# Sorted edge records scattered as rows of 16 words into tables of 64-byte rows

## What is computed

```
x = x + gnn0(norm(x), src, dst)        # two layers: mean of x[dst] over the edges of src, dense, norm, silu
x = x + experts(norm(x))               # 8 experts, two per node, 256 -> 1024 -> 256
x = x + gnn1(norm(x), src, dst, w)     # sum of w * x[src] over the edges of dst, dense, norm, gelu
x = x + half(x)                        # top half of each block of 512 rows through a dense pair
```

## Time and profile before

| | us |
|---|---|
| median of 3 runs | 7271.44 |
| lowest and highest | 7270.54, 7273.53 |
| span of the profiled execution | 7265.6 |
| busy in it: TensorE | 3646.1 |
| POOL | 3769.2 |
| VectorE | 2657.8 |
| ScalarE | 899.9 |

### The profile page before, as it was taken

One profiled execution on the slowest core, in us unless ns is written; L12 is line 12 of the kernel. 1 busy time (PEld: TensorE's weight loads), 2 busy tenths in 40 slices (PEclk: granted clock), 3 DMA queues, 4 the chain that ended last, 5 costly groups with the idle time before them and its releaser, 6 DMA issues. The chain is left out here.

```text
span 7265.6 us, 61921 instructions
## 1 busy us (share of the span) xinstructions
PE 3646.1 (50%) x13991; PEld 2632.2 (36%) x13992; DVE 2657.8 (37%) x6350; ACT 899.9 (12%) x2400; POOL 3769.2 (52%) x3797
## 2 busy tenths in 40 slices
PE   4112974444544445444431222299992455555729
PEld 1001543333333333333221000178881334333517
DVE  5115864444433444444340000011114455555661
ACT  0000950000003000000230000022221100000322
POOL 4772036666663666666537777700005566666321
PEclk7556987777777777777665555599996678787859
DMA  3000113333321333332011000022214233333250
GB/s 136 1 0 30 21 49 92 92 92 92 91 61 61 90 92 91 92 92 83 21 58 59 4 2 8 4 75 81 83 57 137 88 90 91 90 91 91 70 162 18
DMA packets 290147, 497.59 MB, mean 68 GB/s; under 512 B 99253, under 2 KB 182880, under 8 KB 290048
## 3 DMA queue, kind: packets, MB, share of 16 engines
q0 software_dynamic: 163264, 345.19, 16.7%
q1 hardware_dynamic: 125696, 150.28, 6.3%
q10 hardware_dynamic: 1088, 1.05, 0.1%
HBM read 487.50 MB, written 92.89 MB: 80 GB/s over the span
## 5 line engine op out<-in xcount | busy, mean ns | idle before, releaser
L970 PE MATMUL sum_sums<-sum_got,sum_onehot 128*128 x4992 | 1613.7, 484 | 1690.7 <-DVE acc L1132 1360.6
L902 POOL DMA_INDIRECT sum_got<-xn,edge_row x1568 | 1541.5, 983 | 1138.9 <-issue 451.4
L970 PEld LDWEIGHTS sum_sums<-sum_got,sum_onehot 128*128 128x128 f32 x4992 | 1166.3, 244 | 2121.9 <-issue 1915.4
L1132 DVE TENSOR_TENSOR acc<-acc,sum_sums 128x257 f32 (+1 forms) x2496 | 1052.7, 422 | 1777.8 <-remote 1241.3
L902 POOL DMA_INDIRECT sum_got<-h,edge_row x784 | 754.4, 962 | 453.3 <-issue 228.4
L1270 POOL DMA_INDIRECT table<-rec,addr x784 | 802.8, 1024 | 298.5 <-issue 277.4
L1866 PE MATMUL moe_f_ps_y<-xb,moe_f_hT 128*128 128x256 f32 x1792 | 478.8, 399 | 317.3 <-issue 317.2
L1850 PE MATMUL moe_f_ps_h<-moe_f_xT,xb 128*128 128x256 f32 x1792 | 473.1, 396 | 303.9 <-issue 303.9
L1931 DVE TENSOR_TENSOR moe_f_y<-moe_f_ps_y,moe_b 128x256 f32<-128x256 f32 x112 | 42.4, 420 | 1362.4 <-DMA table<-acc 718.5
L1698 POOL DMA_INDIRECT moe_out_c_got<-moe_out,place_i x98 | 95.0, 970 | 824.5 <-PEq L1656 785.1
L1270 POOL DMA_INDIRECT table<-sort_rec,sort_addr x392 | 400.0, 1020 | 201.8 <-issue 122.9
(11 more groups left out here) (460 smaller groups left out, 3297.0 us busy)
## 6 DMA issues: line engine op xcount, KB each, us to landing
xb<-in_L_ffn_W SPq DMA_DIRECT2D x112, 1024.0 KB
sum_got<-xn,edge_row POOLq DMA_INDIRECT x1568
moe_in<-acc SPq DMA_DIRECT2D x28, 512.0 KB
moe_f_xin<-moe_in SPq DMA_DIRECT2D x56, 256.0 KB
moe_out<-moe_f_y SPq DMA_DIRECT2D x56, 256.0 KB
xn<-xb SPq DMA_DIRECT2D x14, 896.0 KB
table<-rec,addr POOLq DMA_INDIRECT x784
sum_got<-h,edge_row POOLq DMA_INDIRECT x784
```

The costliest lines, as they stand in the source:

```text
L902: pool.indirect_dma_start(got[:, c % SU, 0:D], None, source, bass.IndirectOffsetOnAxis(ap=p.edge_row[:, c:c + 1], axis=0)).then_inc(s_got[ ...
L970: mm = nc.tensor.matmul(sums[k % 2][j], onehot[:, (k % QUARTERS) * HALF + j, :], flat(got[:, bass.ds(where[n % PLAN], 1), :]), start=True, ...
L1132: v.tensor_tensor(a, a, sums[k % 2][j], ALU.add).then_inc(s_added[j], 1)
```

## The change

Both tables get rows of WIDE = 16 words, 64 bytes, so 6.42 MB each for 0.40 and 0.80 MB. A scatter sends, for each of its 128 records, the 16 words from the record's own word on: the record, and then what follows it in the partition (the next columns' records), which nobody reads. For that the record buffers are 16 words longer than their columns, cleared by two memsets. The number of scatters and of rows in each stays.

The fills write the wide tables from the same small buffer, repeated by a stride of zero; table0's is ahead of the load of x, table1's behind it with a semaphore of its own, which is waited for at the end of SP's program in the stage. POOL waits for the first alone. The readback brings all 16 words of each row to the chip (`raw`), and only word 0 (and 1) is used. Since `raw` fills the scratch room, what is made from it overlays it or goes elsewhere, the unpacking is in another order with a wait between, and a memset moves to a later function.

```diff
--- before.py
+++ after.py
@@ -55,6 +55,7 @@
 KEYBITS = 13
 NONE = P
 LOWBITS = 9
+WIDE = 16
 LOW = 1 << LOWBITS
 EX = 8
 TOP = 2
@@ -148,7 +149,8 @@
         lane = p.sb("lane", [P, EC], I32, ctx)
         local = p.sb("local_sh", [P, EC], I32, ctx)
         addr = [p.sb("addr0", [P, EC], I32, ctx), p.addr1]
-        rec = [p.sb("rec0", [P, EC], I32, ctx)[:], p.rec1[:, :, 0]]
+        records = [p.sb("rec0", [P, EC + WIDE], I32, ctx)[:], p.rec1[:].rearrange("p c f -> p (c f)")]
+        rec = [records[0][:, 0:EC], p.rec1[:, 0:EC, 0]]
 
 
         running, base_i = pos_i[:].bitcast(F32), lane
@@ -184,7 +186,8 @@
         s_const, s_keys0, s_keys1, s_keyfill = s("s_const"), s("s_keys0"), s("s_keys1"), s("s_keyfill")
         s_dve, s_addr, s_fill, s_prefill = s("s_dve"), s("s_addr"), s("s_fill"), s("s_prefill")
         s_zero, s_xpad, s_x, s_xnout = s("s_zero"), s("s_xpad"), s("s_x"), s("s_xnout")
-        scatter = Scatter(p, ctx, dram["table0"], addr[0], rec[0].unsqueeze(2))
+        scatter = Scatter(p, ctx, dram["table0"], addr[0], records[0], 1)
+        s_prefill1 = s("s_prefill1")
         s_wload, s_wT, s_wcopied = s("s_wload"), s("s_wT"), s("s_wcopied")
         s_pool, s_small = s("s_pool"), s("s_small")
         s_lane, s_scaled, s_hot, s_placed, s_whole = (
@@ -225,7 +228,7 @@
             nc.gpsimd.iota(p.node_no[:], [[P, NT]], base=0, channel_multiplier=1,
                            allow_small_or_imprecise_dtypes=True).then_inc(s_const, 1)
 
-            pool.wait_ge(s_prefill, 32)
+            pool.wait_ge(s_prefill, 16)
             pool.wait_ge(s_addr, 1)
             scatter.run(pool, 0, SENT)
 
@@ -274,11 +277,14 @@
             sp.wait_ge(s_keyfill, 3)
             load(weight, io["edge_weight"], s_keys1)
             sp.wait_ge(s_fill, 1)
-            sp.dma_start(dram["table0"].rearrange("(p q) a -> p (q a)", p=P), fill[:, 0:QW]).then_inc(s_prefill, 16)
-            sp.dma_start(dram["table1"].rearrange("(p q) a -> p (q a)", p=P), fill[:, :]).then_inc(s_prefill, 16)
+            repeats = QW * WIDE // (2 * QW)
+            empty = fill.unsqueeze(1).to_broadcast([P, repeats, 2 * QW])
+            tables = [dram[f"table{k}"].rearrange("(p r q) a -> p r (q a)", p=P, r=repeats) for k in range(2)]
+            sp.dma_start(tables[0], empty).then_inc(s_prefill, 16)
             sp.wait_ge(s_xpad, 1)
             sp.dma_start(xb[:, 0:NT - 1, :], tiles(io["x"], 0, NT - 1)).then_inc(s_x, 16)
             sp.dma_start(xb[0:LAST, NT - 1, :], rows(io["x"], NT - 1, LAST)).then_inc(s_x, 16)
+            sp.dma_start(tables[1], empty).then_inc(s_prefill1, 16)
 
             sp.wait_ge(s_zero, 1)
             zeros = 0
@@ -300,6 +306,7 @@
                     small += 1
             sp.wait_ge(s_small, 16 * small)
             sp.wait_ge(s_zero, 1 + 16 * zeros)
+            sp.wait_ge(s_prefill1, 16)
 
         @block.tensor
         def _(pe):
@@ -463,6 +470,8 @@
             nc.vector.memset(fill, NONE << KEYBITS).then_inc(s_fill, 1)
             nc.vector.memset(xb[:, NT - 1, :], 0.0).then_inc(s_xpad, 1)
             nc.vector.memset(zero, 0.0).then_inc(s_zero, 1)
+            c.done(nc.vector.memset(records[0][:, EC:], 0))
+            c.done(nc.vector.memset(records[1][:, 2 * EC:], 0))
             c.done(nc.vector.memset(p.ones[:], 1.0))
             c.done(nc.vector.memset(p.eps[:], EPS))
             c.done(nc.vector.memset(ones_row, 1.0))
@@ -489,7 +498,7 @@
             tile_numbers(0)
             count(0)
             dve.wait_ge(s_keys1, 96)
-            c.done(nc.vector.tensor_copy(p.rec1[:].bitcast(F32)[:, :, 1], weight))
+            c.done(nc.vector.tensor_copy(p.rec1[:, 0:EC, :].bitcast(F32)[:, :, 1], weight))
             c.link(nc.vector.tensor_tensor(rec[0], local[:], key[1][:], ALU.bitwise_or))
             rank(0)
             part = slice(0, SENT)
@@ -776,8 +785,8 @@
                 at += width
                 return room[0:of, at - width:at]
 
-            raw = take(CH * fields).bitcast(I32).rearrange("p (q a) -> p q a", a=fields)
-            dense = [take(CH) for k in range(fields)]
+            raw = room[:, 0:CH * WIDE].bitcast(I32).rearrange("p (q a) -> p q a", a=WIDE)
+            dense = [take(CH), p.edge_weight[:, 0:CH]][0:fields]
             dense_flip = [take(BLOCKS * P, BLOCK) for k in range(fields)]
             chunk, place, above, below = (take(PIECES) for k in range(4))
             reach = [min(BLOCK + NT, PIECES - BLOCK * b) for b in range(BLOCKS)]
@@ -796,7 +805,7 @@
                                       "s_kept_flip", "s_low", "s_high"))
             s_pick, s_picked, s_plan, s_placed, s_zeroed = (
                 s("u_" + x) for x in ("s_pick", "s_picked", "s_plan", "s_placed", "s_zeroed"))
-            early = 2 * fields * CH
+            early = CH
             parts = [(0, 512), (512, PIECES)]
             count_row = banks[1][0:1, PIECES - 512:PIECES - 512 + CH // EU]
         block = ctx.enter_context(nc.Block())
@@ -1000,19 +1009,22 @@
                 if not weighted:
 
                     c.link(v.tensor_tensor(whole, whole, raw[:, :, 0], ALU.add))
-                    c.link(v.tensor_copy(raw[:, :, 0], whole))
-                v.tensor_single_scalar(p.edge_row[:], raw[:, :, 0], (1 << KEYBITS) - 1, ALU.bitwise_and).then_inc(s_table, 1)
-                c.link(v.tensor_single_scalar(local_i, raw[:, :, 0], KEYBITS, ALU.arith_shift_right))
-                v.tensor_copy(dense[0], local_i).then_inc(s_dense, 1)
+                    c.link(v.tensor_copy(local_i, whole))
+                else:
+                    c.link(v.tensor_copy(local_i, raw[:, :, 0]))
+                v.tensor_single_scalar(p.edge_row[:], local_i, (1 << KEYBITS) - 1, ALU.bitwise_and).then_inc(s_table, 1)
                 if weighted:
                     v.tensor_copy(dense[1], raw[:, :, 1].bitcast(F32)).then_inc(s_dense, 1)
+                    dve.wait_ge(s_dense, 1)
+                dve.wait_ge(s_table, 1)
+                c.link(v.tensor_single_scalar(local_i, local_i, KEYBITS, ALU.arith_shift_right))
+                v.tensor_copy(dense[0], local_i).then_inc(s_dense, 1)
 
             def ends_of_tiles(c):
 
 
                 whole, at_start, at_end = cell[0:NT, 0:2], cell[0:NT, 2:3], cell[0:NT, 3:4]
                 number = p.chunk_no[0:NT, :]
-                c.done(v.memset(nothing, 0.0))
                 c.link(v.tensor_copy(cell_i[0:NT, :], p.bounds[0:NT, order, :]))
                 c.link(v.tensor_single_scalar(cell_i[0:NT, :], cell_i[0:NT, :], 7, ALU.arith_shift_right))
                 c.done(v.tensor_copy(whole, cell_i[0:NT, :]))
@@ -1028,6 +1040,7 @@
             def tiles_of_pieces(c):
 
                 number = p.chunk_no[0:NT, :]
+                c.done(v.memset(nothing, 0.0))
                 v.tensor_scalar(counts, p.ones[0:NT, :], cell[0:NT, 4:5], None, ALU.mult).then_inc(s_started, 1)
                 v.tensor_scalar(started, number, cell[0:NT, 2:3], None, ALU.is_ge).then_inc(s_started, 1)
                 dve.wait_ge(s_tiles, 1)
@@ -1253,9 +1266,9 @@
 class Scatter:
 
 
-    def __init__(self, p, ctx, table, addr, rec):
-
-        self.p, self.table, self.addr, self.rec = p, table, addr, rec
+    def __init__(self, p, ctx, table, addr, words, fields):
+
+        self.p, self.table, self.addr, self.words, self.fields = p, table, addr, words, fields
         self.s_sent = [p.sem(f"sc_s_sent{h}", ctx) for h in range(FLYING)]
 
     def run(self, pool, first, end):
@@ -1268,7 +1281,7 @@
                 pool.wait_ge(self.s_sent[h], sent[h])
             sent[h] += 16
             pool.indirect_dma_start(self.table, bass.IndirectOffsetOnAxis(ap=self.addr[:, c:c + 1], axis=0),
-                                    self.rec[:, c, :], None, bounds_check=limit,
+                                    self.words[:, self.fields * c:self.fields * c + WIDE], None, bounds_check=limit,
                                     oob_is_err=False).then_inc(self.s_sent[h], 16)
         for h in range(FLYING):
             pool.wait_ge(self.s_sent[h], sent[h])
@@ -1279,7 +1292,7 @@
 
 
 def second_scatter(p, ctx):
-    return Scatter(p, ctx, p.table1, p.addr1, p.rec1)
+    return Scatter(p, ctx, p.table1, p.addr1, p.rec1[:].rearrange("p c f -> p (c f)"), 2)
 
 
 BANKS, FLIPS, PUTS = 4, 2, 4
@@ -2298,7 +2311,7 @@
 
 def build(nc, io, out):
     dram = {name: nc.dram_tensor(name, shape, dt).ap() for name, shape, dt in (
-        ("table0", (P * QW, 1), I32), ("table1", (P * QW, 2), I32), ("xn", (NT * P, D), F32),
+        ("table0", (P * QW, WIDE), I32), ("table1", (P * QW, WIDE), I32), ("xn", (NT * P, D), F32),
         ("h1", (NT * P, D), F32), ("x2", (NT * P, D), F32),
         ("moe_in", (MOE_TILES * FT, D), F32), ("moe_out", (MOE_TILES * FT + P, D), F32),
         ("pair", (NT * P, 2 * D), F32))}
@@ -2313,7 +2326,7 @@
 
         p.edge_row = p.sb("edge_row", [P, CH], I32)
         p.edge_local, p.edge_weight = (p.sb(n, [P, PIECES + PLAN]) for n in ("edge_local", "edge_weight"))
```

(2 more changed lines are left out.)

## The result

The changed kernel took 7302.8 us (median of 5, 7292.4 to 7310.95) beside 7271.33 us (median of 5, 7266.24 to 7273.53) for the kernel before: ratio 1.0044, 95% interval 1.0031 to 1.0056. It is slower by 31.5 us. The forecast was 6000, in a range from 5940 to 7000; rival A's time was 7307.

The account below looks back on a forecast made before the run. Bound: the service time of 4- and 8-byte scatter rows, in four stretches summing to about 1658 us. Forecast 7271.4 - 377 (sort) - 75 (gnn0) - 83 (gnn1) - 772 (experts) + 36 (readbacks) = 6000 us, range 5940 to 7000.

Parts of the forecast that it names:

- rival A: All four scatter stretches: 64-byte rows are served like the small ones, only readbacks add, 7307 us; chance 0.16.
- What bounds the kernel: Four scatter stretches: service time of 4- and 8-byte rows, about 1.41 us per scatter, sums to about 1658 us.
- 1.417 with a drain of 33.6 us: Sort: service time per 128-row scatter, from VectorE's masks being back at pace at 637.9, 33.6 us after the last issue.
- The scatter itself: All scatters: a 64-byte-row scatter costs what a 1-KB one does, at most 1.288 us for 1.417; given 74%.
- the 11 us to the next stage: After the 98 scatters of 1-KB rows: next stage starts about 11 us after the last; added to POOL's forecast chains.
- 4 and 8 bytes cost the same, so it is a small write as such: Small-row scatters: 1.417 and 1.400 us, so the price was taken as one of a small write, not of bytes.
- the gaps on issue in the last stage: TensorE among 2-KB gathers: "issue" gaps of 1.73 us, put down to large transfers that pile up.
- The queue: Scatter stretches: a queue a tenth short makes every engine stand, and had to drain after the last issue.
- The free pace of the four stretches: Sort, gnn0, gnn1, experts: if the queue keeps up, the longer chain sets each; gains 377, 75, 83 and 772 us.
- Readbacks: Two table readbacks, 6.42 MB each for 0.40 and 0.80: about +18 us each, +36, from 30 to 48.
- Fills: Filling the wide tables: 11.6 MB more to write, 32 us at 359 GB/s, all hidden.

Follow-up runs that it names:

- The probes: Kernel before plus indirect DMAs behind the experts' scatters: 400 of five kinds, 7832.0 us beside 7313.2; or scatters at several paces, 5970.1 beside 5542.6 and 7415.4 beside 7300.0.
- paced kernels: Kernel before with a memset on POOL behind scatters: 16 words, 7071.9 us beside 7300.0 or 5634.1 beside 5542.6; longer pauses, 6343.4, 6205.8 and 6164.9 us.
- the free execution: Kernel before plus memsets and scatters at several paces behind the experts' scatters, in a comparison without starved engines: 5970.1 us beside 5542.6.
- Segment b: 80 scatters of 128 rows of 1 KB, up to 49 in flight, among 400 indirect DMAs added to the kernel before: 7832.0 us beside 7313.2.
- the second probe's segment e: 60 scatters of 16 rows, added with other paces behind the experts' scatters of the kernel before, run starved: 7415.4 us beside 7300.0; scatters 1.147 us apart.
- its a: 50 scatters of 128 rows, each with a 16-word memset behind it, in the same starved kernel, 7415.4 us beside 7300.0; scatters 1.388 us apart.

## Why the prediction was wrong

*What bounds the kernel* was half right: engines that wait for nothing the profile shows, beside POOL's DMAs, and something that takes 1.40 us per scatter while POOL offers one per 1.28. The probes and paced kernels bear out that figure and that POOL's margin over it was all that mattered. The other figure, 1.417 with a drain of 33.6 us, was a misreading: the group of the earlier trace rows was cut at 638, and the masks are back at their pace from 631.67 on, 27.4 us behind the last scatter, which gives (631.7 - 82.4) / 392 = 1.40 for the sort too.

*The scatter itself* is the step that failed. I took "what a 1-KB row does, at most 1.288 us" from the earlier trace rows as the lower end, and then as the value. But 1.288 us is how fast POOL issued them; it is 1.28 for the starved small ones too. Behind the first 10 us no other engine had work in that stretch that could have been seen to stand. Nor do the 11 us to the next stage say that there was no drain: the free execution has the same (3072.7 to 3084.6, as 3862.3 to 3874.2), so they belong to the change of stage, and a lag of 98 x (1.40 - 1.288) = 11 us would just hide in them. I had held a pace of issue for a time of service. Segment b showed it: 1-KB rows starve TensorE to 20% and are served in the same 1.40 us. The argument "4 and 8 bytes cost the same, so it is a small write as such" had the other reading beside it, that size doesn't enter at all. A row for it was at hand: the gaps on issue in the last stage, among gathers of 2 KB. The prediction put them down to large transfers that pile up; the free execution, with the same transfers, has none.

*The queue.* "A queue was behind and had to drain" left open what was queued; the forecast counted on rows that are served faster, so on the transfers. Two in flight changed nothing, so it is something tied to the instruction, not to the data. What it is stays open.

*The free pace of the four stretches* was right. The sum had 615, 107, 139 and 846 us (the sort's readback at 615, the others as lengths from the first scatter); the free execution has 604, 106.4, 143 and 837. The gain that the forecast counted, 1307 us, is there, 1323, but it comes with an execution that doesn't starve, not with wider rows. What the forecast left out is that the gathers starve as well, 360 us.

*Readbacks*: +36 forecast, within 30 to 48; 30.7 measured (16.1 and 14.6). The first transfer is used 18.4 us behind its issue, 348 GB/s with the latency in, so the rate was right; but the small tables had not been as cheap as their bytes (1.1 and 2.2 us): they came into use 2.8 and 4.5 us behind the issue. *Fills*: hidden, as said; the first scatter is at 82.1 for 82.4.

*Rival A* had the time: 7307 forecast, 7302.8 measured. That 64-byte rows are served like the small ones is so; its reason, that a write of under some size is slow, is not, since rows of 1 KB are no faster. It had a chance of 0.16, and no row of the trace before settled which of the two readings of the earlier trace rows held. The range left it out.

## What to carry to other kernels

The pace at which an engine issues doesn't yet say how fast its instructions are served, and a stretch in which nobody else works can't show that nobody is held up; before a resource is called "kept up with", there must be an engine in that stretch that would show it. Where engines idle on "issue" beside a stream of indirect DMAs, vary the stream's pace first: a pause of 0.25 us behind each one took 15% off this kernel where it starved (a shorter one cost 1.6% where it didn't), while the bytes, the rows and the number in flight took nothing. And repeat a comparison at another time or on another chip before the cause is sought in the kernel alone.

## What the runs showed of the hardware

Indirect DMAs that POOL issues one per 1.39 us or faster hold up TensorE, VectorE, ScalarE and POOL's own next instructions in some executions and not in others: the same kernel took 5542.6 us in one comparison and 7262 to 7322 us in the rest (but for one execution of 8914.9, of which there is no profile). Under the same chip number, 4, it was free once and starved once. It is a price per instruction, 1.40 us: 16 rows or 128, 4 bytes or 1 KB, scatter or gather, all leave TensorE 20% busy at POOL's full pace, one matmul per 2.80 us; with one offered per 1.39 us it was 45 to 49%. It is paid late: TensorE ran on for 14 us (the second probe's segment e) to 23 us (its a) after the start, and the engines were held up for some 27 us after the last of a long stream. At 1.53 us and more between them nothing was held up. Which part of the chip this is, and what makes one execution starve and another not, these runs don't tell; that two in flight starve it as much as 49 speaks against the transfers themselves. The free probe's scatters took, from issue to landing:

```profile
DMA to landing us min/median/max: 1.9/2.1/2.2
```

The Trainium skill ("DMA: Bandwidth & Descriptors", Anatomy of one DMA) gives about 2.0 us as the fixed cost of a DMA that GpSimd issues, up to its completion, and the trace agrees with its 2.1.
